# Attention and mixture of experts on one core: a new prologue order, transposes in another bank, value tiles after their attend, and float32r halves for the expert down products

## The reference

```
q, k, v = xn @ W_Q + b_Q, xn @ W_K + b_K, xn @ W_V + b_V      # 16 heads of 128
z = softmax(causal(q k^T / sqrt(128))) v;  attention = z @ W_O + b_O

x1 = rmsnorm(xn) * ln1_w                                       # the ffn's own attention
q, k = rotary(x1 @ wq), rotary(x1 @ wk); v = x1 @ wv           # 16 heads, 4 key/value heads
r = xn + softmax(causal(q k^T / sqrt(128))) v @ wo
xf = rmsnorm(r) * ln2_w
probs = softmax(xf @ gate_w^T); top 4 of 32 experts, weights renormalised
moe = sum over the chosen e of w_e * (silu(xf @ weg[e]) * (xf @ weu[e])) @ wed[e]
ffn = r + moe + (silu(xf @ wsg) * (xf @ wsu)) @ wsd
```

## Time and profile before

| | |
|---|---|
| median of 3 runs | 773.32 us (771.32 to 773.82) |
| profiled execution | 773.67 us, span on the core 771.8 us |
| TensorE busy | 745.4 us, 97% of the span, 4641 products |
| DVE busy | 547.1 us, 71% |
| ACT busy | 488.8 us, 63% |
| POOL busy | 478.1 us, 62% |
| HBM traffic | 51.36 MB read, 24.69 MB written |

### The profile page before, as it was taken

One profiled execution on the slowest core, in us unless ns is written; L12 is line 12 of the kernel. 1 busy time (PEld: TensorE's weight loads), 2 busy tenths in 40 slices (PEclk: granted clock), 3 DMA queues, 4 the chain that ended last, 5 costly groups with the idle time before them and its releaser, 6 DMA issues. The chain is left out here.

```text
span 771.8 us, 14397 instructions
## 1 busy us (share of the span) xinstructions
PE 745.4 (97%) x4641; PEld 663.2 (86%) x4641; DVE 547.1 (71%) x1687; ACT 488.8 (63%) x1218; POOL 478.1 (62%) x553
## 2 busy tenths in 40 slices
PE   7789899999999999999989999999999999999997
PEld 4578788888889899888878889999999999999986
DVE  5888888887979787766688667655556565555574
ACT  2677677787778776568354665655566565566652
POOL 5658577777867696335363774466564766656553
PEclk8999999999999999999999999999999999999999
DMA  6000000100011079700101462476877777667634
GB/s 194 8 15 28 14 15 15 35 15 22 15 42 42 15 227 278 187 14 15 42 15 47 101 201 84 98 177 162 202 177 166 182 177 171 145 156 168 126 56 142
DMA packets 102691, 76.99 MB, mean 100 GB/s; under 512 B 6918, under 2 KB 101466, under 8 KB 102618
## 3 DMA queue, kind: packets, MB, share of 16 engines
q1 hardware_dynamic: 91426, 62.74, 28.6%
q0 software_dynamic: 10608, 12.61, 10.3%
q10 hardware_dynamic: 584, 0.73, 0.3%
HBM read 51.36 MB, written 24.69 MB: 99 GB/s over the span
## 5 line engine op out<-in xcount | busy, mean ns | idle before, releaser
L695 POOL TENSOR_SCALAR probs<-probs,inv_sum 128x128 f32<-128x128 f32 x240 | 141.2, 604 | 152.7 <-DVE inv_sum L1464 147.5
L1185 ACT ACTIVATE probs<-probs,neg_max 128x128 f32<-128x128 f32 (+3 forms) x256 | 143.0, 559 | 121.6 <-DVE neg_max L1458 120.3
L868 PE MATMUL s<-k_heads,q_heads 128*128 128x256 f32 (+2 forms) x576 | 138.8, 362 | 3.3 <-DVE neg_max L1458 3.0
L1458 DVE CUSTOM_DVE_ANT_0 probs<-s,mask 128x128 f32<-128x128 f32 (+3 forms) x256 | 120.0, 485 | 16.7 <-PE s L868 10.7
L757 POOL DMA_INDIRECT moe_sum_dram<-late,slot_tokens x63 | 99.2, 1574 | 38.2 <-ACT late L1273 26.5
L1473 DVE TENSOR_TENSOR probsT<-t,probsT 128x384 fp32r<-128x384 f32 (+2 forms) x192 | 101.2, 548 | 12.9 <-ACT probsT L1200 12.5
L1200 ACT ACTIVATE probsT<-t 128x384 fp32r<-128x384 f32 (+2 forms) x192 | 90.1, 488 | 18.5 <-PE t L1010 18.3
L868 PEld LDWEIGHTS s<-k_heads,q_heads 128*128 128x128 f32 x576 | 91.2, 190 | 9.6 <-DVE neg_max L1458 5.9
L1010 PE MATMUL t<-ident,probs 128*128 128x128 f32 x640 | 94.5, 274 | 3.1 <-POOL probs L695 2.3
L1010 PEld LDWEIGHTS t<-ident,probs 128*128 128x128 f32 x640 | 74.8, 140 | 12.6 <-POOL probs L695 4.4
L868 PE MATMUL zb<-probsT,v_heads 128*128 128x512 f32 (+2 forms) x351 | 68.9, 340 | 1.4 <-DVE probsT L1473 0.9
(11 more groups left out here) (258 smaller groups left out, 1592.2 us busy)
## 6 DMA issues: line engine op xcount, KB each, us to landing
x_slots_dram<-mask SPq DMA_DIRECT2D x1, 8480.0 KB, 38.1
late<-x_slots_dram SPq DMA_DIRECT2D x32, 265.0 KB, 4.4
late<-in_L_ffn_weg_dram SPq DMA_DIRECT2D x63, 128.0 KB
late<-in_L_ffn_weu_dram SPq DMA_DIRECT2D x63, 128.0 KB
late<-in_L_ffn_wed_dram SPq DMA_DIRECT2D x63, 128.0 KB
moe_sum_dram<-mask SPq DMA_DIRECT2D x2, 1152.0 KB, 8.2
raw_qk<-in_L_ffn_wq_dram SPq DMA_DIRECT2D x16, 128.0 KB, 2.2
raw_o<-in_L_ffn_wo_dram SPq DMA_DIRECT2D x8, 256.0 KB, 2.7
```

The lines of the kernel that those rows point to most:

```text
L695: pool.tensor_scalar(piece, piece, rinv[:, u % 2, i:i + 1], 1.0, ALU.mult, ALU.mult).then_inc(p_norm, 1)
L868: m = pe.matmul(dst, lhs(a), rhs(b), start=first and i == 0, stop=last_ and i == 2, skip_group_check=skip)
L1185: act.activation(piece, piece, ACT.Exp, bias=nmax[:, u % 2, i:i + 1], scale=-1.0, accum_out=rsum[:, u % 2, i:i + 1]).then_inc(e_done, 1)
L1458: ve.tensor_tensor_reduce(pr[:, u % 2, P_OFF[i]:P_OFF[i] + width], bS[i % 2][:, 0:width], mask_t[:, S - width:S], INV_SCALE, BIG, ALU.add, ...
```

## The change

It has four parts.

1. **Prologue.** The filler products become four of 512 columns ahead of the constants and three of 128 behind the first turns. ACT loads its table first, waits for x's second half before it issues the transfers of the rope table and the biases, and writes the high halves of the first K/V weights; POOL writes only their low halves, and waits for the rms rows first. DVE takes the statistics of x's second half ahead of the first evictions. The first Krope product is ordered so that the four products with high halves of x come first. In unit -2 POOL's `q_sin` comes ahead of the power of the second half, Qrope 0's low half moves to DVE, and the four rms rows of the second half are made one at a time: one before that low half, one after, two behind the first masks of unit -1.
2. **Normal rows.** XN goes into bank zb. In the first half's units `over_from` comes behind Q's projection and the first two blocks of scores, its eviction on ACT behind the first two exponentials, on DVE behind the third mask. `normal_row` makes one row tile behind the masks and one ahead of z.
3. **Value tiles.** In units 30 to 40 (`stays`) the third chunk is projected behind the unit's own attend (`third_of`) and evicted behind z. Four operations of the router move from unit 38 to unit 39.
4. **Expert down products.** ACT and DVE split each pair's down weights (`down_hi`, `down_lo`, 128x512 each) and, once a unit, the inner values of both pairs (`inner_hi`, `inner_lo`, 128x512); Y is made by `mm3` from these halves and waits for them.

Some buffers change places in memory for that (the shared expert's weights share space with the new halves, the constant rows and b_O with buffers of the second half).

```diff
     def over_from(n):
-        return chunks_of(n - 1)[2:] if 0 < n <= UNITS else []
+        return chunks_of(n - 1)[2:] if 0 < n <= UNITS and not stays(n - 1) else []
+    def stays(n):
+        return HALF - 2 <= n < UNITS and not pairs_of(n)
+    def third_of(n):
+        return chunks_of(n)[2:] if stays(n) else []
...
-            return over_from(n) + own[:1] + out + [("Z", n)] + own[1:]
+            return own[:1] + over_from(n) + out + [("Z", n)] + own[1:]
...
-                at = 2 if ch[0] == "Z" else 3
+                at = 3 if ch[0] == "O" else 2
...
# POOL
+                if job == ("KV", 0):
+                    pool.wait_ge(ln_step, LN["xr", TB - 1])
+                else:
+                    for hi, _, raw in parts:
+                        last = pool.tensor_scalar(hi, raw, 1.0, 1.0, ALU.mult, ALU.mult)
+                    last.then_inc(w_hi, 1)
...
                     if n == -2 and job[0] == "Q3":
+                        q_sin(n, it)
                         first_powers(1)
-                        q_sin(n, it)
-                        q_lo(n, it)
...
# TensorE
-            keep_busy(3)
+            keep_busy(4, S)
...
-            keep_busy(1)
+            keep_busy(3, P)
...
+                else:
+                    r = ch[1]
+                    pe.wait_ge(dn_lo, r - SHARED + 1)
+                    pe.wait_ge(h_lo, (r - SHARED) // 2 + 1)
+                    for j in blocks_of(r):
+                        m = mm3(dst[:, j * D:(j + 1) * D], lambda p: hs[:, p, r % 2, j, :],
+                                lambda p: ds[:, p, r % 2, j * D:(j + 1) * D], j == 0, j == blocks_of(r)[-1], skip=True)
...
-                if rotary:
-                    for ch in over_from(n) + (chs[:1] if n else []):
-                        project(ch, it)
+                if rotary and n:
+                    project(chs[0], it)
                 if nxt:
                     scores(n + 1, 0, it)
                     scores(n + 1, 1, it)
+                if rotary:
+                    for ch in over_from(n):
+                        project(ch, it)
...
+                    for ch in third_of(n):
+                        project(ch, it)
                     guests(n, 5)
...
# ACT
+            act.wait_ge(x_in[1], 16)
             act.dma_start(rope_t[:, :], rope_table).then_inc(rope_in, 16)
...
+            half = KD * P
+            act.wait_ge(raw_in["KV"], 32)
+            for (hi, _, raw) in first_parts(half):
+                last = act.activation(hi, raw, ACT.Copy)
+            last.then_inc(w_hi, 1)
...
+            def down_hi(n, i):
+                for r in pairs_of(n)[i:i + 1]:
+                    if r >= SHARED:
+                        act.wait_ge(wr_in[(r - SHARED) % 3], 96 * ((r - SHARED) // 3) + 48 * len(blocks_of(r)))
+                        act.wait_ge(j_mm, CHUNK["Y", max(r - 2, SHARED - 1)] + 1)
+                        act.activation(ds[:, 0, r % 2, :], wdn[(r - SHARED) % 3].rearrange("p j d -> p (j d)"),
+                                       ACT.Copy).then_inc(dn_hi, 1)
+            def inner_hi(n):
+                rs = pairs_of(n)
+                if rs and rs[0] >= SHARED:
+                    kept(act, ("G", rs[0]))
+                    kept(act, ("G", rs[1]))
+                    act.activation(hs_t[:, 0:4 * P], hb_t, ACT.Copy).then_inc(h_hi, 1)
...
                     normalise(n, (0, 1))
+                    down_hi(n, 0)
...
                     normalise(n, (2,))
+                    down_hi(n, 1)
                     for ch in chs[:2]:
                         chunk_a(ch, it)
+                    inner_hi(n)
                     normalise(n, (3,))
...
                     z_part(n, it)
+                    for ch in third_of(n):
+                        chunk_a(ch, it)
...
# DVE
-                        rms_rows(1)
+                        rms_rows(1, (TB,))
+                        ve.wait_ge(rp_hi["Qrope"], 1)
+                        ve.tensor_tensor(qT[:, 0, 1], rot_sum(q)[:, P:S], qT[:, 0, 0].bitcast(f32),
+                                         ALU.subtract).then_inc(rp_lo["Qrope"], 1)
+                        rms_rows(1, (TB + 1,))
...
                     times_up(n, 3)
+                    down_lo(n, 0)
...
                     times_up(n, 4)
+                    down_lo(n, 1)
                     guests(n, 4)
                     route_m(n)
                     for ch in chs[:2]:
                         chunk(ch, it)
+                    inner_lo(n)
                     z_part(n, it)
+                    for ch in third_of(n):
+                        chunk(ch, it)
                     route_1(n)
...
+                normal_row(n, 0)
                 invert(n + 1, 2, it)
...
-                normal_rows(n)
+                normal_row(n, 1)
                 z_part(n, it)
...
                     then(ve.tensor_reduce(rsm[:, 3], weights, AX.X, ALU.add))
+                if n == RANKS + 1:
+                    weights = x2r[:, :, D + 1 + TOPK:ROW]
                     then(ve.tensor_scalar(rsm[:, 0], rsm[:, 3], 1e-12, None, ALU.max))
```

More of the change, by code:

```diff
@@ L433, in vacant, with first_parts @@
                 until(eng, taken[BANK[ch]], NTH[ch], it, BANK_W[BANK[ch]])
+        def first_parts(half):
+            kk = lambda ap: ap[:, 0:half].rearrange("p (k w i) -> p k w i", k=KD, w=2)
+            return [(kk(wkvA[:, 0]), kk(wkvA[:, 1]),
+                     rkv_t[:, 0:half].rearrange("p (k i w) -> p k w i", k=KD, w=2)),
+                    (wkvA[:, 0, half:2 * half], wkvA[:, 1, half:2 * half], rkv_t[:, half:2 * half])]
         def windows(eng, step):
@@ L889, in project @@
                     off = 0 if kind == "Krope" else half
-                    for k in range(KD):
-                        if ch == ("Krope", 0):
-                            pe.wait_ge(x_lo, k + 1)
+                    if ch == ("Krope", 0):
+                        for i, (p, r, k) in enumerate([(0, 0, 0), (1, 0, 0), (0, 0, 1), (1, 0, 1), (0, 1, 0), (0, 1, 1)]):
+                            if r == 0:
+                                pe.wait_ge(x_hi, k + 1)
+                            else:
+                                pe.wait_ge(x_lo, k + 1)
+                            m = pe.matmul(dst[:, :], wkvA[:, p, k * P:(k + 1) * P], xrT[:, r, k, 0:S],
+                                          start=i == 0, stop=i == 5)
+                    for k in range(KD if ch != ("Krope", 0) else 0):
                         m = mm3(dst[:, :], lambda p: wkvA[:, p, off + k * P:off + (k + 1) * P],
@@ L1357, in step @@
                     return
-                for ch in over_from(n) + chs[:1]:
-                    chunk_a(ch, it)
+                chunk_a(chs[0], it)
                 exp(n + 1, 0, it)
                 exp(n + 1, 1, it)
+                for ch in over_from(n):
+                    chunk_a(ch, it)
                 probs_hi(n, 2, it)
@@ L1636, in step @@
                     return
-                for ch in over_from(n):
-                    chunk(ch, it)
                 k_product, k_last = behind(n, 1, "Krope"), behind(n, 2, "Krope")
@@ L1732, in times_up, with down_lo, inner_lo @@
                                          ALU.mult).then_inc(taken[BANK[ch]], 1)
+            def down_lo(n, i):
+                for r in pairs_of(n)[i:i + 1]:
+                    if r >= SHARED:
+                        ve.wait_ge(dn_hi, r - SHARED + 1)
+                        ve.tensor_tensor(ds[:, 1, r % 2, :], wdn[(r - SHARED) % 3].rearrange("p j d -> p (j d)"),
+                                         ds[:, 0, r % 2, :].bitcast(f32), ALU.subtract).then_inc(dn_lo, 1)
+            def inner_lo(n):
+                rs = pairs_of(n)
+                if rs and rs[0] >= SHARED:
+                    ve.wait_ge(h_hi, (rs[0] - SHARED) // 2 + 1)
+                    ve.tensor_tensor(hs_t[:, 4 * P:], hb_t, hs_t[:, 0:4 * P].bitcast(f32), ALU.subtract).then_inc(h_lo, 1)
             fetched = [0]
```

70 lines of the change are left out of this document (35 added, 35 removed).

## The result

| | before | after |
|---|---|---|
| median of 4 runs, us | 772.35 | 782.55 |
| lowest to highest, us | 771.32 to 773.82 | 780.07 to 783.05 |
| profiled execution, us (span) | 773.67 (771.8) | 782.99 (780.7) |

The changed kernel is slower: ratio 1.0128, 95% interval 1.0101 to 1.0155, 9.9 us. 778.0 us was forecast, with a range of 770.5 to 784.5 us: a loss of 4.7 us against the measured 9.9. The sign and the main cause held; the size of the loss was forecast at less than half. In the profiles the losses of the experts and of the value tiles and the gain of XN came out larger than forecast, the gain of the prologue smaller.

What follows compares the result with a forecast made beforehand. TensorE was taken as the bound, so only its work or waits count. From 773.67 us, +8.9 (experts) - 2.0 (XN) + 2.1 (value tiles) - 4.4 (prologue) gave 778.3, 778.0 us on the median's level; range 770.5 to 784.5.

Steps and rivals of the forecast that it cites:

- Experts, +8.9 forecast: Expert units: Y waits 0.85 us for inner_lo sixteen times, 13.6 us, less 4.7 us from faster down products.
- Rival 1: At Y behind attend: halves ready when attend ends, wait costs 0 instead of 13.6 us, 764.3 us; chance 0.11.
- Rival 4: Expert units: new DVE subtractions stretch beside POOL, 0.4 us more per unit, +6.4 us, 784.4 us; chance 0.04.
- XN, -2.0 forecast: Normal rows' transposes, moved later and to z's bank, lose waits of up to 3.6 us; -2.0 us taken (0 to -3.6).
- what is late next is DVE: Normal rows: DVE's nearly unbroken chain keeps two row operations (1.51 us) and the eviction, so -2.0 instead of -3.6 us.
- Value tiles, +2.1 forecast: Units 30 to 40: V's eviction behind z delays squares and router arithmetic, outweighing vanished waits; +2.1 us (-3.5 to +4).
- the router's: Router units: V's low half comes between z and DVE's arithmetic: +1.1, about 0, -0.5, +0.1 and -0.6 us.
- Rival 2: Units 30 to 40: value tiles' old waits go, new ones are hidden, -3.5 instead of +2.1 us, 772.4 us; chance 0.10.
- Prologue, -4.4 forecast: Prologue: held clock, Q's low half on DVE and earlier masks gain, later transfers cost; -4.4 us (-6 to -1).
- The mask step: Prologue: three of four row operations (3.64 us together) move behind DVE's masks, which come earlier; 1.9 us gained.
- If the clock holds, up to 1.8 us: Prologue's six first products, 3.31 us mostly at 1.2 GHz: a fourth filler covers the wait ahead, saving up to 1.8 us.
- Rival 3: The prologue gives nothing, since ACT is held by the late x: 782.4 us; chance 0.09.

Runs made afterwards that it cites:

- experiment 4: Changed kernel with inner_hi and inner_lo moved ahead of K's eviction on ACT and DVE; ratio to the kernel before 0.9918.
- experiment 10: Changed kernel with h's halves ahead of K's eviction, value tiles put back, and first K/V weights' high halves back on POOL; ratio to before 0.9856.
- Experiments 7 and 11: Changed kernel, h's halves before K's eviction, old value tiles. 7: XN transposes in old place, 0.9889; 11: XN's two row operations together, 0.9895 (to before).
- experiment 6: Changed kernel with h's halves ahead of K's eviction and V's eviction moved behind the next head's probabilities; ratio to before 0.986.
- experiment 2: Kernel before with the expert part alone added; ratio to before 1.0135.
- experiment 8: Changed kernel with h's halves ahead of K's eviction, value tiles put back, and the old prologue fillers; ratio to before 0.9867.
- Experiment 9: Changed kernel, h's halves before K's eviction, old value tiles, four row operations of x's second half together ahead of head 0's masks; ratio to before 0.986.
- experiments 1 and 3 to 6: Changed kernel with: 1, expert part undone, 0.9986; 3, value tiles put back, 1.0068; 5, that plus h's halves before K's eviction, 0.9866; others listed separately.

## Why the prediction was right, and where it was off

**Experts, +8.9 forecast, +10.3 measured.** Every link was as told: place, releaser, sixteen times, 0.72 us per pair, 0.30 us gained per unit, down_hi and down_lo free. The term that was too small is the wait, 0.95 us per unit (17.10 - 16.15) instead of 0.85: 16 x 0.1 = 1.6 us. Counted from the start of attend's last product, inner_lo was forecast to end at 0.96 us (510.07 - 509.11) and Y to start at 1.06; in the changed kernel they are at 0.96 (509.29 - 508.33) and 1.11 us. What I took off was too much: Y's old start at 0.22 us, where a float32r Y can start at 0.13 (experiment 4). Rival 1 (halves ready when attend ends) is what experiment 4 made true, and its price was near: no wait, a faster kernel (0.9918 of 772.35 us is 766.0 us, 764.3 forecast). Its break-even of 0.55 us per unit could not be tried apart. Rival 4 (stretched subtractions) did not come about. One of three DVE subtractions per unit is stretched, the second down_lo with 1.03 us, and it hides: experiment 4 has the full gain with that row in it. Here the Trainium skill, GPSIMD Engine Reference, section Specifications, says that POOL shares its SBUF interfaces with VectorE. This case's rows agree that there is a price, and show it on either side: POOL's alone in the earlier trace rows, DVE's 0.35 us here (1.03 against 0.68 us) and 1.2 us in experiment 10.

**XN, -2.0 forecast, -3.8 measured**, beyond the forecast's own end. The step that failed is "what is late next is DVE". The upper bound of 3.6 us, the two waits of the earlier trace rows, was the right number. Timeline of the changed kernel, TensorE in unit 5, where before stood a wait of 1.13 us for the bank and then one of 1.5 us for the rows:

```profile
75.03 0.60 PE L886 MATMUL s<-k_heads,q_heads 128*128 128x256 f32 x3
75.47 0.60 PE L923 MATMUL zb<-ident,acc_a 128*128 128x128 f32 x4
75.82 0.95 PE L886 MATMUL ob<-w_o,zT 128*128 128x256 f32 x6
```

Neither the transposes nor the out projection wait. I had called DVE's chain nearly unbroken without a row for it; in this unit DVE stands for 1.46 us ahead of the third mask, so the eviction found most of its room. The lateness that I feared is there but small: attend waits for the low half behind that eviction 0.30 us in this unit (before 0), and 1.37 us in unit 1 (before 0.93). I had taken 1.6 us off the upper bound for it. Experiments 7 and 11 show a part of where the gain sits: the place, given the new bank, 1.9 us, the split rows 0.6 us; the rest goes to the bank by subtraction only.

**Value tiles, +2.1 forecast, +5.4 measured**, the largest error, and beyond the forecast's own end of +4 (within it, at +3.8, without the 1.6 us of clock told below). Where the squares are the forecast was near: 2.0 us against 2.65 us (units 31 to 35). The step that failed is the router's: +0.1 us was forecast for its five units 36 to 40, +1.1 of it in the first, and +2.7 us came, 2.3 of them in unit 36. The chain was as told, here at 333 to 339 us:

```profile
334.23 0.60 ACT L1283 ACTIVATE v_heads<-j 128x512 fp32r<-128x512 f32 x1 [0.70 <-PE j L886]
334.73 0.41 ACT L1199 ACTIVATE vT<-acc_a 128x256 f32<-128x256 f32 x1
...
338.24 0.28 DVE L1524 CUSTOM_DVE_ANT_0 probs<-s,mask 128x128 f32<-128x128 f32 x1
...
337.78 0.44 PE L1039 MATMUL t<-ident,probs 128*128 128x128 f32 x2 [0.70 <-DVE probsT L1539]
338.59 1.49 PE L886 MATMUL s<-k_heads,q_heads 128*128 128x384 f32 x6 [0.36 <-DVE neg_max L1524]
```

The squares start 2.2 us behind attend (V's product starts at 332.56), 2.05 us forecast, and the unit lost 0.85 us (0.95 forecast, though its own working, 343.65 - 342.75, gives 0.90), in two waits and not in one. In unit 36 the +1.1 us was put on DVE's arithmetic behind z. What the rows show instead is 0.7 us of the same lateness, reaching the router's inputs: the transposes and logits wait 0.35 and 0.51 us for ACT's scaled rows and their eviction. The other 1.6 us are TensorE's lower clock, for which there was no term and which the same program also ran without (experiment 4); they are chance at least in part and are not to be read as the order's price. Rival 2 (the value tiles pay) is wrong for the change as made. With the eviction moved (experiment 6) they come out level with the old order, clock apart.

**Prologue, -4.4 forecast, -3.1 in this pair.** The mask step was right in kind: the row operations behind the masks shorten the stretch to head 1 from 9.55 to 7.46 us, 2.1 us against 1.9 us forecast. But in the profile of before TensorE's clock is at 1.2 GHz for 3.4 us of that stretch, from 26.4 us on. In experiment 2, which has the old prologue and no such fall, it is 8.70 us: there the gain is 1.2 us. Two steps failed. "If the clock holds, up to 1.8 us": it held, 1.67 us for the products of 3.31, but TensorE then stood 1.74 us for w_kv. Against the 3.4 us at the low level in experiment 8 the fillers are worth nothing; against the 6.8 us in the profile of before they may be worth more, as its first scores stand at 23.38 us and those of experiment 2, with the same prologue and 3.4 us, at 22.20. And the first scores, which waited 0.99 us for POOL's low half of Q, now wait 1.46 us for DVE's:

```profile
12.76 1.67 PE L914 MATMUL j<-xrT,w_kv 128*128 128x512 f32 x6 [1.74 <-POOL w_kv L704]
...
22.39 0.46 PE L1024 MATMUL s<-k_first,rope_sum 128*128 128x128 f32 x2 [1.46 <-DVE q_heads L1644]
...
28.79 1.09 PE L1039 MATMUL t<-ident,probs 128*128 128x128 f32 x8 [0.27 <-POOL probs L714]
```

DVE's low half begins when ACT's high half is there, not when the row operation ahead of it in DVE's queue ends:

```profile
21.21 0.93 DVE L1644 TENSOR_TENSOR q_heads<-rope_sum,q_heads 128x384 fp32r<-128x384 f32 x1 [0.16 <-ACT q_heads L1352]
```

Experiment 9, which takes that operation away, has the same wait of 1.46 us ahead of the first scores. So DVE's queue does not hold the first scores. The path through ACT and the subtraction itself do, which takes 0.93 us on DVE and took 0.99 us on POOL.

The transposes stood at 31.86 us; 27.5 us was forecast, 28.79 us it is. The stage also scatters: with the old prologue the scores of head 1 start at 32.93 and 30.90 us in two traces, with the new one at 28.75 to 30.18 us in those of the changed kernel and of experiments 1 and 3 to 6. The 2.0 us between the two old ones go with the clock, 10.2 us at 1.2 GHz in the one and 3.4 us in the other. So the term is about -2.5 us, give or take 1, and a difference of 1 us in it from one pair of traces is no evidence. Rival 3 (it gives nothing) is out.

**The sum.** -3.1 - 3.8 + 5.4 + 0.1 + 10.3 = 8.9 us, the difference of the spans. The forecast sum was +4.6 us. The four errors, +1.3, -1.8, +3.3 and +1.4 us, come to +4.2 us, nearly the forecast change itself; that 782.55 us lies inside the range is owed to the range's width and to XN's error, which took 1.8 us off. Two terms also hold the clock of the two profiled executions: some 1.6 us of the value tiles' +5.4 and up to 2.0 us of the prologue's -3.1. Each term has to be read by itself before the sum is called right.

## What to carry to other kernels

A new operation that another engine waits for is priced by what stands ahead of it in its own queue: the same two operations behind K's eviction cost 0.95 us sixteen times, and one place earlier nothing. If a forecast finds such a wait, look at once for an idle stretch of that queue behind the operand and ahead of the slow neighbour; it was 0.8 us wide here and in the rows all along. The same holds for an eviction put between two links of a chain: move the product if TensorE has room, and leave its eviction behind the chain.

## What the runs showed of the hardware

- A stall costs from start to start: 0.98 us between attend and Y, of which the bracket of the timeline shows 0.72.
- TensorE's clock fell to 1.2 GHz at or behind the 32 logit products (128x32) and stayed there for 3.4 us (eight traces), for 6.8 us (two), or did not fall at all (three), between traces of which some have the same program in that unit. From 0 to 3.4 us, and from 3.4 to 6.8 us, the unit grew by 1.6 us each (16.31 against 14.72, 18.68 against 17.06).
- Four 128x256 row operations of DVE took 2.58 us with POOL splitting weights beside them and 1.38 us without; one 128x512 subtraction in three took 1.03 instead of 0.68 us.
- On each of the three chips of the experiments the kernels lost about 25 us in one stretch, in which POOL alone went on; in the two profiles of the result they did not. The cause is open. Unit lengths away from the stretch were not touched by it.
